# A decoder layer with mixture of experts: how ScalarE's expert code is laid out, and how expert results are stored, fetched, combined and finished

## What is computed

```
logits = flat_x @ Wg + bg                     # 2048 tokens, 4 experts
top_vals, top_idx = top_k(logits, 2)          # two choices per token, softmax over them
for i in range(4):
    sel_p, sel_idx = top_k(score of expert i, 512)     # an expert takes at most 512 tokens
    tok = flat_x[sel_idx]
    h = gelu(tok @ W1[i]);  y = h @ W2[i] * p          # 512 -> 2048 -> 512
    out = out.at[sel_idx].add(y)
```

## Time and profile before

| what | value |
|---|---|
| median of 3 runs | 1045.03 us (1043.53, 1045.03, 1048.1) |
| the profiled execution | 1047.94 us |
| its span (first to last instruction) | 1046.2 us |
| mean granted TensorE clock | 0.939 of full speed |
| busy: TensorE, VectorE, ScalarE, GpSimd | 89%, 67%, 44%, 46% of the span |

### The profile page before, as it was taken

One profiled execution on the slowest core, in us unless ns is written; L12 is line 12 of the kernel. 1 busy time (PEld: TensorE's weight loads), 2 busy tenths in 40 slices (PEclk: granted clock), 3 DMA queues, 4 the chain that ended last, 5 costly groups with the idle time before them and its releaser, 6 DMA issues.

```text
span 1046.2 us, 19083 instructions
## 1 busy us (share of the span) xinstructions
PE 931.7 (89%) x7297; PEld 555.2 (53%) x7297; DVE 702.9 (67%) x1310; ACT 455.4 (44%) x764; POOL 481.3 (46%) x551
## 2 busy tenths in 40 slices
PE   3588999999999999999999762189989999999995
PEld 2445666667676766766676432044444444444342
DVE  6767788878887788778786747675644445345672
ACT  3445655566556655665556434022332333233210
POOL 1447676767677676767774310201260001003643
PEclk9688999999999999999999875579999999999998
DMA  9413000000000000000000006213253234325593
GB/s 292 132 51 129 4 17 17 5 17 17 14 3 17 17 14 17 3 17 14 17 3 14 12 11 251 82 39 121 84 158 121 83 120 160 104 97 197 158 243 126
DMA packets 40300, 78.39 MB, mean 75 GB/s; under 512 B 11378, under 2 KB 11650, under 8 KB 40258
## 3 DMA queue, kind: packets, MB, share of 16 engines
q1 hardware_dynamic: 35266, 63.13, 18.2%
q0 software_dynamic: 4992, 14.70, 5.3%
HBM read 64.16 MB, written 13.65 MB: 74 GB/s over the span
## 4 chain that ended last, share of the span: by engine, by line
PE 74%; DVE 7%; POOL 4%; issue 4%; DMA 4%; SPq 3%; ACT 2%; POOLq 0%; DVEq 0%; ACTq 0%
PE ps L1091 18%; PE ps L1093 17%; PE ps L1092 17%; PE ps L1097 6%; PE ps L1184 4%; PE ps L1281 3%; PE ps L1263 3%; POOL y_fetched L756 2%; PE ps L1290 2%; PE ps L1310 1%; DVE big L1866 1%; SPq L474 1%; PE ps L1196 1%; DMA y_fetched<-y_scratch,idx_get 1%; POOL hrs L604 1%
## 5 line engine op out<-in xcount | busy, mean ns | idle before, releaser
L1064 ACT ACTIVATE big<-ps 128x512 f32<-128x512 f32 x64 | 38.2, 597 | 239.3 <-PE ps L1093 225.5
L604 POOL TENSOR_TENSOR hrs<-hve,neg_half 128x16 f32<-128x16 f32 x43 | 125.6, 2922 | 3.4
L1963 DVE TENSOR_SCALAR big<-big 128x512 f16<-128x512 f32 x64 | 27.7, 432 | 118.6 <-ACT big L1064 106.5
L1091 PE MATMUL ps<-w2h,big 128*128 128x512 f16 x256 | 98.4, 384 | 5.0 <-DVE big L1488 5.0
L1091 PE MATMUL ps<-big,w1h 128*128 128x512 f16 x256 | 98.0, 383 | 1.4 <-DVE big L1488 1.4
L1093 PE MATMUL ps<-w2h,big 128*128 128x512 f16 x256 | 98.4, 384 | 0.0
L1092 PE MATMUL ps<-w2l,big 128*128 128x512 f16 x256 | 98.4, 384 | 0.0
L1092 PE MATMUL ps<-big,w1h 128*128 128x512 f16 x256 | 97.8, 382 | 0.0
L1093 PE MATMUL ps<-big,w1l 128*128 128x512 f16 x256 | 97.8, 382 | 0.0
L739 POOL DMA_INDIRECT big<-x_scratch,token_of x16 | 18.2, 1138 | 154.0 <-PE ps L1097 82.3
L756 POOL DMA_INDIRECT y_fetched<-y_scratch,idx_get x32 | 36.8, 1149 | 105.4 <-issue 98.9
(11 more groups left out here) (311 smaller groups left out, 2481.5 us busy)
## 6 DMA issues: line engine op xcount, KB each, us to landing
wst<-in_w SPq DMA_DIRECT2D x28, 1024.0 KB
x_scratch<-xn SPq DMA_DIRECT2D x16, 256.0 KB, 2.1
y_fetched<-in_w SPq DMA_DIRECT2D x4, 1024.0 KB, 13.4
out<-x_all SPq DMA_DIRECT2D x4, 1024.0 KB, 8.7
pr<-in_w_attn SPq DMA_DIRECT2D x3, 1024.0 KB, 8.6
x_all<-in_w_attn SPq DMA_DIRECT2D x3, 1024.0 KB, 11.2
x_all<-in_x SPq DMA_DIRECT2D x1, 3072.0 KB, 11.7
y_scratch<-big SPq DMA_DIRECT2D x3, 1024.0 KB, 5.9
```

Of the source, the lines that this page charges most:

```text
L604: pool.tensor_tensor(hrs[n][:, :], hve[n][:, :], neg_half[:, :], ALU.pow).then_inc(hdev[n], 1)
L1064: act.activation(hg[f % 2], psum[f % 2][:, 512:1024], ACT.Gelu, scale=UN).then_inc(hg_r, 1)
L1091: nc.tensor.matmul(o, lh, rh, start=first, stop=False)
```

## The change

Four things, in one edit. ScalarE's experts 1 and 2 are written out (other engines keep the loop). Results of an expert are stored in four transfers of 256 KB, each after its own tile. All fetches of a group, first and second choice, count one semaphore per group, a combine waits for its own group alone, and combining begins in step 4: 3, 5, 3, 5 sequences in steps 4 to 7 for the first choice, and four each in steps 8 to 11 for the second. In the last expert, the products of chunks 14 and 15 come in the order 14: t0, t1, t2; 15: t0, t1; 14: t3; 15: t2, t3.

```diff
             def store_results(e):
-                sp.wait_ge(y_ev, 4 * (e + 1))
-                sp.dma_start(y_dram[bass.ds(e * CAP, CAP), :].rearrange("(t p) d -> p t d", p=P), y_sb).then_inc(y_st, 16)
+                for t in range(CAP // P):
+                    sp.wait_ge(y_ev, 4 * e + (t + 1))
+                    sp.dma_start(y_dram[bass.ds(e * CAP + t * P, P), :], y_sb[:, t, :]).then_inc(y_st, 16)
...
-            pool.wait_ge(y_st, 16 * (E - 1))
+            pool.wait_ge(y_st, 16 * (CAP // P) * (E - 1))
             for b in range(B):
-                fetch(0, b, lo_in)
+                fetch(0, b, y_in[b // (B // NG)])
             for g in range(NG):
                 pool.wait_ge(comb, (g + 1) * (B // NG))
                 for b in range(g * (B // NG), (g + 1) * (B // NG)):
-                    fetch(1, b, hi_in[g])
+                    fetch(1, b, y_in[g])
...
-            with act.Fori(1, E - 1) as e:
+            for e in range(1, E - 1):
                 expert(e, True)
...
+            def down_tile(f, t):
+                hf, fc = f // FH, f % FH
+                tk = slice(t * P, (t + 1) * P)
+                return mm3(psum[2 + t // 2][:, (t % 2) * 512:(t % 2 + 1) * 512], hh[f % 2][:, tk], hl[f % 2][:, tk],
+                           w2h[hf][:, fc, :], w2l[hf][:, fc, :], f == 0, f == 2 * FH - 1)
+
+            def down_last():
+                f = 2 * FH - 1
+                pe.wait_ge(hl_r, E * 2 * FH - 1)
+                for t in range(3):
+                    down_tile(f - 1, t)
+                pe.wait_ge(hl_r, E * 2 * FH)
+                for t in range(2):
+                    down_tile(f, t).then_inc(h_used, 1)
+                down_tile(f - 1, 3)
+                down_tile(f, 2).then_inc(h_used, 1)
+                down_tile(f, 3).then_inc(half_used[1], 1)
...
                     if not more and LO_STEP <= f < LO_STEP + NG:
-                        for b in range((f - LO_STEP) * (B // NG), (f - LO_STEP + 1) * (B // NG)):
-                            combine(0, b, lo_in, 16 * B)
+                        for b in range(LO_FROM[f - LO_STEP], LO_FROM[f - LO_STEP + 1]):
+                            combine(0, b)
...
-            LO_STEP = 2 * FH - 2 * NG - 3
-
-            def combine(k, b, fetched, count):
-                dve.wait_ge(fetched, count)
+            LO_STEP = 2 * FH - 2 * NG - 4
+            LO_FROM = (0, 3, 8, 11, B)
+
+            def combine(k, b):
+                dve.wait_ge(y_in[b // (B // NG)], 16 * (B // NG) * (k + 1))
```

More of the change, by code:

```diff
@@ L326, in decoder_layer @@
         y_ev, y_st = sem("y_ev"), sem("y_st")
-        lo_in, hi_in, comb, out_st = sem("lo_in"), sems("hi_in", NG), sem("comb"), sem("out_st")
+        y_in, comb, out_st = sems("y_in", NG), sem("comb"), sem("out_st")
         slot_put, slot_in, part_in, last_st = map(sem, ("slot_put", "slot_in", "part_in", "last_st"))
@@ L1428, in up, with down @@
                 last.then_inc(h_ps, 1)
-            def down(e, f, final=False):
+            def down_tile(f, t):
[14 more added lines that the diff above has]
+                down_tile(f, 3).then_inc(half_used[1], 1)
+            def down(e, f):
                 n = e * (2 * FH) + f
@@ L1437, in down @@
                 for t in range(4):
[L1438 to L1442, removed]
+                    last = down_tile(f, t)
                 if fc == FH - 1:
@@ L1462, in expert @@
                             token_turn(e + 1, t)
-                    down(e, f, not more and f == 2 * FH - 1)
+                    if more or f < 2 * FH - 2:
+                        down(e, f)
+                if not more:
+                    down_last()
             token_list(0)
@@ L1972, in last_results @@
             def last_results():
-                dve.wait_ge(y_st, 16 * (E - 1))
+                dve.wait_ge(y_st, 16 * (CAP // P) * (E - 1))
                 dve.wait_ge(part_in, 16 * (CAP // P))
@@ L1977, in last_results @@
                     if t < 3:
-                        dve.wait_ge(h_used, E * (2 * FH - 2) + t + 1)
+                        dve.wait_ge(h_used, E * (2 * FH - 2) - 1 + t + 1)
                     else:
@@ L1986, in results @@
                 if not isinstance(e, int) or e >= 1:
-                    dve.wait_ge(y_st, 16 * e)
+                    dve.wait_ge(y_st, 16 * (CAP // P) * e)
                 for t in range(4):
@@ L2016, in expert @@
                         for b in range(g * (B // NG), (g + 1) * (B // NG)):
-                            combine(1, b, hi_in[g], 16 * (B // NG))
+                            combine(1, b)
                 if more:
```

## The result

The changed kernel takes **1040.48 us** (median of 18 runs, 1035.69 to 1047.23) against 1044.53 (18 runs of the kernel before on the same chip, 1040.02 to 1050.64): ratio **0.9955, 95% interval 0.9937 to 0.9973**, or 4.05 us less. The forecast was 1040.3 us and -0.45%.

What follows compares the result with a forecast made beforehand. TensorE is nearly full in the expert stage, so only its gaps and the end after its last matmul count. 0 + 0 + 4.10 + 0.59 = 4.7 us off the median 1045.03 gives 1040.3 us, range 1036.5 to 1044.5.

Steps and rivals of the forecast that it cites:

- Gap A: Between experts 0 and 1: TensorE idles 2.75 us, its release to ScalarE late; bound 4.6 us, no gain counted.
- Part 1: ScalarE's middle experts written out: loop costs under 0.1 us, hidden by slack; worth 0.
- Part 2: Expert 2's results stored by tiles: last quarter lands 2.2 us earlier for expert 3's fetches; worth 0 by itself.
- Part 3: Expert 3: fetches combined by groups, one step sooner, remove VectorE's wait and TensorE's idle time; gain 4.10 us.
- Gap B: Expert 3: VectorE waits 6.72 us for all 16 first-choice fetches, TensorE idles 2.25 us, clock drops; costs 4.10 us.
- cover of 3.0 us at step 11: Expert 3, second choice: last fetch landed by 1008.5 at worst; TensorE notices only combines beginning after 1011.5.
- worst landing: Slowest fetch landing in the first profile, 8.71 us, taken as the worst case for expert 3's fetches.
- R2: Rival, chance 0.12: TensorE idles at step 11 or 12 of expert 3 for late second-choice fetches; 1041.5 to 1044 us.
- Part 4: Last two chunks by tiles: first eviction starts at 1032.95 instead of 1033.54; gain 0.59 us, 0 if partial rows stay late.
- The sum: Whole kernel: all four parts together take 4.7 us off, span 1046.2 to 1041.5.
- R3: Rival, chance 0.08: expert 3's stall is much smaller in unprofiled runs, nothing measurable beyond noise; 1044 to 1045 us.
- R4: Rival, chance 0.07: slower, as more and earlier stores and fetches cause new late TensorE releases, 4.6 us each; 1049.5 us.

Runs made afterwards that it cites:

- e1: Kernel before with only ScalarE's experts 1 and 2 written out; 1046.16 us against 1045.16, ratio 1.001.
- e2: Changed kernel with ScalarE's loop over experts 1 and 2 put back; 1039.77 us, ratio 0.994 to the kernel before.
- e8: Changed kernel with combines moved back to the old steps 5 to 12, four each; 1043.96 us against 1050.06 for the kernel before, ratio 0.9945.
- e10: Changed kernel unchanged, timed beside the one with old combine steps on one chip; 1045.34 us against 1050.06 for the kernel before, ratio 0.9964.
- e0: Kernel before, unchanged, run once more for its profile; 1050.87 us in its one execution.
- e7: Changed kernel, unchanged, run once more for its profile; 1039.84 us in its one execution.
- e5: Changed kernel with expert results stored in 1 MB transfers again; 1042.2 us, ratio 0.9967 to the kernel before.
- e3: Kernel before with only fetches counted and combined by groups, one step sooner; 1042.21 us against 1045.16, ratio 0.9983.
- e9: Kernel before with only the new order of the last two chunks; 1053.54 us in its one execution.
- e6: Changed kernel with the last two chunks in the old order; 1041.67 us, ratio 0.9959 to the kernel before.
- e4: Kernel before with combines waiting by groups, but in the old steps 5 to 12, four each; 1040.65 us against 1045.31, ratio 0.997.
- e11: Kernel before with group waits in the old steps and the new last-chunk order, loop and 1 MB stores kept; 1040.22 us against 1044.77, ratio 0.9954.

## Why the prediction was right, step by step

**Gap A.** Right that the lateness is ahead of ScalarE and not its loop (e1, e2, e8, e10). Right, too, that other runs have less of it: 4 profiles of 14 have it. Wrong that the fastest run is what this one would be without it: e0 has no gap A and took 1050.87 us, because its experts begin 7 us later. Why TensorE's release comes late isn't settled. It has come at this place in both forms of the kernel; beyond that I argued only from what GpSimd and SyncE do there, and no run changed that. I overlooked that the four profiles with gap A are also the only ones whose trace is incomplete (last section), so the gap may belong to the recording and not to the kernel. The Trainium skill (Runtime: NRT & Kernel Launch, Instruction fetch mechanics) speaks for unrolling because of the fetch after a taken branch; no run here shows such a cost, in the pair e1 and e2 or in the traces: the 0.08 us at the loop's entry are no more than the register step ahead of the GELU.

**Part 1, 0 us.** Right: 1.001 alone, and 0.994 for the changed kernel without it.

**Part 2, 2.2 us sooner, worth 0.** The size is right. The last quarter landed 2.31 us after its issue (chain of e2 and e7), a whole store 4.42 to 4.49. The first fetch begins 3.65 us after expert 3's first GELU (949.74 - 946.09) against 5.65 before, 2.0 us sooner. It then takes 1.94 us on GpSimd instead of 1.00, so nearly half is given back at once. Worth 0 is right with the combines in their old steps; with the new ones the store may have a part in the cover below (e5, e3).

**Part 3, 4.10 us.** The place is right; the size was one profile's. Gap B took 4.10 and 3.88 us in before and e9, but 2.87 in e0 and e1, with almost the same wait of VectorE (6.72, 6.51, 6.44 and 6.45 us). The difference is the clock, shown in a window of e0 right behind the idle time:

```profile
989.00:993.00 4.00, 4.00 (x19) 1.79 (x20) 4.00 (x5) 0.00 (x0) 3.39 (x3) 1.00 0.36 88
```

In e0 TensorE idled 1.97 us, and 0.57 us once more a chunk later, and the next 4 us ran at 1.00; in before it idled 2.25 us and they ran at 0.57. What is not lost there is in part lost later, for the partial rows do not come sooner with it: the tails of e0 and e1 are 17.82 and 17.31 us against 16.09. The loss in expert 3 and the tail together come to 20.2, 20.7 and 20.2 us in before, e0 and e1, and to 15.6, 16.7 and 15.6 us in the three profiles of the changed kernel. So a gain of 4.10 in expert 3 and 0.59 behind it became in e0's terms 2.87 in expert 3 and 2.3 behind it, with nearly the same sum. That the sum held is partly luck: the prediction didn't know of this trade.

The step that failed inside part 3 is the cover of 3.0 us at step 11. It was made of two sizes, both too small. The last fetch was to begin at 999.8; it began at 997.71 - 946.1 + 950.9 = 1002.5 on that axis, 2.7 us late. The second pass starts 1.0 us late (974.19 is 979.0 there, not 978), and it is issued in (997.71 - 974.19) / 15 = 1.57 us each, not 1.45, which makes 1.8. That alone takes nearly the whole cover: the fetch then landed in 8.8 us, about what was assumed, and the combines, which have to begin by 1011.5 - 950.9 + 946.1 = 1006.7 on the changed kernel's axis, began at 1006.55 (above). 0.15 us was left, and that it was enough is luck. The second size is the landing: in e2, e3, e5, e6 and e7 the last fetch lands 9.6 to 10.5 us after it begins, not within 8.71. In e0, the kernel before, it took 10.30 as well, and the last combine waited 2.10 us for it, so the "worst landing" was the worst of one execution, and not a bound. In e7, the same kernel as after, there was no cover left (chain, then timeline):

```profile
946.55 2.31 DMA y_scratch<-big
...
997.50 10.52 DMA y_fetched<-y_scratch,idx_get
```
```profile
1008.04 2.74 DVE L2048 SCALAR_TENSOR_TENSOR x_all<-y_fetched,wk,x_all 128x512 f32<-128x512 f32 x4 [3.72 <-DMA y_fetched<-y_scratch,idx_get]
...
1011.99 0.38 PE L1092 MATMUL ps<-w2h,big 128*128 128x512 f16 x1 [0.95 <-DVE big L1506]
```

So R2 is real, in small: it takes back 0 to 1.1 us in the changed kernel, in some executions and not in others. Its price of 1.8 us for each us idle was too high: e7 lost 1.11 us for 0.95 idle, with the granted clock at 1.00 behind it (window of 1012 to 1016 us).

**Part 4, 0.59 us.** 0.48 us measured. The wait that I foresaw ahead of the last chunk's tile 0 is there, with 0.16 us and not 0.2 to 0.3 (the matmul before it starts at 1022.73, and 0.216 us is usual): its first matmul starts at 1023.11, right behind the split's end at 1022.37 + 0.69 = 1023.06. I foresaw the eviction 2.85 us after the last GELU (1028.85 - 1026.0), and it came 1024.09 - 1021.20 = 2.89 after it. The partial rows were to be 3.35 us ahead of it. The last gather begins at 1018.42 and lands 3.77 us later, at 1022.2 (3.64 and 3.81 us in e0 and e1), 1.9 us ahead: the late fetches again.

**The sum, 4.7 us.** 4.05 us measured; the interval of the ratio, 0.27 to 0.63% of 1044.53, makes it 2.8 to 6.6. From the first GELU on, without gap A, 350.4 and 350.9 became 345.8 to 346.9: 3.5 to 5.1 us. R3 was right in that gap B is often smaller, but the tail made up for it; R4 did not come.

## What to carry to other kernels

Where a consumer waits for a whole batch and takes it in pieces, give each piece its own count; that was nearly the whole gain here (e4: 4.2 to 4.7 us from the first GELU on, 0.997 by time). Once that wait is gone, asking a step sooner moves the wait to the last piece: before pulling a consumer forward, work out when the last piece lands, and leave room for more than the slowest landing of one trace (8.71 us there, 8.3 to 10.5 in others). And compare stretches between two fixed events, over several profiles, when a chance stall of the size of the effect lies in some of them.

## What the runs showed of the hardware

**The clock after a stall.** Short idle times of TensorE that differ by little cost quite differently: 1.97 and 1.98 us (e0, e1) and 1.86 and 1.88 us (e8, e10) left the granted clock at 1.00; 2.04 us (e9) and 2.25 us (before) were followed by 4 us at 0.57, near the lower level. The two with the lower clock are also the two in which gap A had come some 200 us before, with 3.35 and 2.75 us idle and a low clock behind it (0.58 and 0.57), so these profiles don't say whether the length of the idle time alone decides. Windows of e9 behind its 2.04 us, and of e8 around its gap A:

```profile
993.00:997.00 4.00, 4.00 (x12) 1.49 (x11) 4.00 (x5) 0.00 (x0) 3.20 (x3) 0.57 0.39 104
```
```profile
778.00:785.00 7.00, 5.14 (x25) 2.16 (x23) 4.44 (x5) 2.88 (x3) 1.01 (x2) 1.00 0.66 248
```

**Late releases.** The gap between experts 0 and 1 cost 4.61 and 5.14 us with 2.75 and 3.35 us of idle time (before, e9), and 2.03 and 2.05 us with 1.86 and 1.88 (e8, e10). It is the largest effect of a single place in these traces, it comes and goes in one and the same program (before and e0; after and e10), and its cause is open. The granted clock stayed at 1.00 in e8's and fell in before's: of the 2.6 us between the two, 0.9 is longer idle time and the rest goes with the clock. e10 has one more late release, in expert 3: a GELU at 1000.56 after 7.11 us idle, 2.5 us late, for which TensorE didn't wait.

What goes with it in all four, and in none of the ten others, is a trace with missing records. The profile gives the median time to landing of the weight pieces in every profile but these four, because semaphore updates that tell of landings are missing there (before, then e0):

```profile
wst<-in_w SPq DMA_DIRECT2D x28, 1024.0 KB
```
```profile
wst<-in_w SPq DMA_DIRECT2D x28, 1024.0 KB, 5.2
```

Counted over the trace, 449 to 507 updates by DMAs are missing in before, e8, e9 and e10, and 13 or 14 in each of the others. Against a complete trace about 120 updates of all kinds are gone by 80 us after expert 0's first GELU, so the loss begins ahead of gap A, which stands at about 84 to 92 us. Whether the recording delays TensorE's releases, or both come of something else, no run shows; a reader should not count gap A as time of the kernel before that is known.

**Indirect fetches under load.** In e0 and e1 the last fetch of the first choice landed 3.70 us after it began, and the last of the second choice, behind which nothing else of GpSimd's was queued, 10.30 and 9.85 us; in the chains of before, e2, e3, e5, e6 and e7 that last fetch has 8.71 to 10.52, in after it took 8.8 and in e4 and e11 8.3 and 8.4. A busy DMA alone doesn't explain it: the second pass of the changed kernel runs at a DMA share of 0.46 and then 0.86 (windows above), but the first pass, whose last fetch landed in 3.7 us, has 0.74 as well (950 to 974 us, 246 GB/s). What the cause is was not tried.

**Open.** The 10 us by which the start of the experts differs among programs that are alike up to there (688.0 to 698.3 us) was not looked into; it is most of the scatter of the times.
